# One core, decay mixing and a routed low-rank layer: the first group's router sums in 64 rows, and other places for its sigmoid, some additions, copies and weight chunks

## The chip, the core and the metric

One core of a Trainium2 chip runs the whole program. Its engines are PE (TensorE, the matrix products), DVE (VectorE), ACT (ScalarE), POOL (GpSimd) and SP (SyncE, which here only issues transfers); each works through its own instructions in order and waits on semaphores. The metric is the device time of one execution in microseconds (us).

## What is computed

The reference, cut to what matters (4 sequences of 1024 steps, 1024 channels, 16 experts of rank 16, a router with 64 hidden values):

```python
ekv = exp(min(k, 30)) * v              # k = v = fside
nf, df = forward decaying sums of ekv, ek over time
nb, db = the same backward in time
euk = exp(min(u + k, 30))
base = sigmoid(r) * ((nf + nb - ekv + euk * v) / max(df + db - ek + euk, 1e-8))
y = base * (0.8 + 0.2 * tf)            # r = x
h = silu(y @ rw1.T + rb1)
logits = (h @ rw2.T + rb2)[:, :16] + gates
coeff = softmax of the two largest logits, at their places
out = x + y @ W.T + bias + einsum(B, (y @ A.T) * coeff)
```

## The kernel before

**Units.** A unit is 128 channels of one sequence over its 1024 steps; there are 32, eight for each sequence (CB is 8). Step s of each engine's main loop deals with unit s and with what is left of unit s - 1. On DVE a unit costs two forward scans (`forward`, `forward_num`), two backward ones (`backward_den`, `backward_num`), `p2`, `sum_den`, `scale_e` for the next unit and, in the next step, `ratio`. ACT takes the exponentials (`exp_k`, `exp_uk`), `sigmoid_r`, and with `inverse` a logarithm and an exponential for the reciprocal, and rounds y to its high part (`split_hi`). The sigmoid is in another function table than the rest, so that ACT loads a table ahead of it and again behind it (`exps`). POOL takes the product `p1`, the sum `sum_n`, the gate `gate_n` and the low part (`split_lo`).

**Groups.** A group is 512 steps of one sequence over its eight units; there are eight, G = 0 to 7, and two of them share a sequence. PE multiplies each y, held as a high and a low part, with weights that are held so too: three products of 512 columns (`three`). For a group it makes the router's sums (`hid`), the two low-rank banks (`low_rank`), the base of outputs j = 0 to 7 (`base`), and the experts' share (`expert`). Between them stands the routing: `hidden`, a sigmoid and `silu`, then `logits` on PE, `routing` on DVE (with one exponential, `exp_gap`, on ACT), `turn` and `spread` on PE with a copy on ACT between (`copy_turned`), `weigh` on DVE, and `split_wx` on ACT and POOL, on which the experts wait.

**Two forms of the router's sum.** `hid` multiplies the weights' high and low parts side by side, 128 rows in all, in two products for a unit; the two halves must then be added, so ACT copies the low rows out (`low_rows`) and DVE adds them (`hidden`). Group 2 (`SPLIT`) uses `hid_sum` instead: three products into 64 rows, with nothing to add, and ACT takes the sigmoid right from the bank (`sigmoid_sum`).

**The order around it.** Hand-written tables say at which step and place each engine does the groups' work: `silu_at`, `routing_at`, `weigh_at` for DVE; `drains_at` for ACT's copies of finished output banks and `adds_at` for POOL's transfers that add them to the output in memory; `x_adds_at` for POOL's transfers that add x; `hi_steps` and `hi_mid_steps` for ACT's half of the weight chunks' split into high and low (POOL's half follows by `lo_steps`); `parts_at` for ACT's copies of part sums. A part is the sum over the first units of one output of group 0 or 1, made while PE has nothing else; `part_depth` says over how many units. There are four buffers for parts, so part 7 goes where part 3 was, once that is stored.

## Time and profile before

| | |
|---|---|
| median of 3 runs | 663.84 us (662.76 to 664.39) |
| the profiled execution | 663.93 us, span 661.9 us |
| mean granted TensorE clock | 0.977 of full |
| busy share of the span | PE 89%, DVE 77%, ACT 56%, POOL 57% |

The span goes from the first to the last instruction; 2.0 us of the execution's own time lie outside it. Matmuls overlap, so that PE counts as busy while they follow each other without a gap.

### The profile page before, as it was taken

The page shows a single profiled execution, that of the slowest core. Times are in us where ns is not written, and L with a number is a line of the kernel's source. Part 1 is how long each engine was busy: PE and PEld are TensorE (multiplying, and loading weights), DVE is VectorE, ACT ScalarE, POOL GpSimd, SP SyncE. Part 2 cuts the span into 40 slices and gives each one's busy share as a digit, 9 for nine tenths or more (in the row PEclk, how much of TensorE's full clock was granted, in tenths as well). Part 3 has the DMA queues.
Part 4 walks back from the last instruction along what each step waited for, and adds up shares of the span by engine and source line. Part 5 has one row for each costly group of instructions (what it writes and reads, how often), then busy time and mean ns, then how long its engine had stood idle before and what let it go on. Part 6 is the DMA issues. An engine that isn't in the chain of part 4 may idle for free.

```text
span 661.9 us, 6944 instructions
## 1 busy us (share of the span) xinstructions
...
## 2 busy tenths in 40 slices
...
GB/s 199 125 95 190 169 200 182 161 161 111 136 78 92 165 125 65 135 213 247 58 143 44 259 79 50 111 175 175 49 111 64 145 0 96 0 159 0 42 55 80
DMA packets 32097, 78.45 MB, mean 119 GB/s; under 512 B 4608, under 2 KB 4800, under 8 KB 32064
## 3 DMA queue, kind: packets, MB, share of 16 engines
...
q8 instruction: 20, 0.33, 0.2%
...
## 4 chain that ended last, share of the span: by engine, by line
PE 45%; DVE 24%; POOL 11%; ACT 7%; issue 7%; DMA 6%; SPq 0%; POOLq 0%; ACTq 0%; DVEq 0%
PE acc L1041 14%; PE acc L1043 14%; PE acc L1042 14%; DVE mix L836 4%; DVE mix L831 4%; DVE mix L827 4%; DVE mix L858 3%; POOL mix L710 3%; DMA yr<-x_cm 2%; POOL y_lo L720 2%; POOL mix L685 2%; DVE eu L846 2%; DVE yr L865 2%; DVE kv L841 1%; POOL yr L691 1%
## 5 line engine op out<-in xcount | busy, mean ns | idle before, releaser
L1041 PE MATMUL acc<-y_hi,wa_hi 128*128 128x512 f32 x638 | 256.6, 402 | 52.4 <-POOL y_lo L720 46.6
L1042 PE MATMUL acc<-y_lo,wa_hi 128*128 128x512 f32 x638 | 253.5, 397 | 0.0
L1043 PE MATMUL acc<-y_hi,wa_lo 128*128 128x512 f32 x638 | 253.4, 397 | 0.0
L1041 PEld LDWEIGHTS acc<-y_hi,wa_hi 128*128 128x128 f32 x638 | 122.9, 193 | 82.9 <-POOL y_lo L720 48.4
L1043 PEld LDWEIGHTS acc<-y_hi,wa_lo 128*128 128x128 f32 x638 | 122.8, 192 | 26.4
L1042 PEld LDWEIGHTS acc<-y_lo,wa_hi 128*128 128x128 f32 x638 | 122.9, 193 | 25.2
L710 POOL TENSOR_TENSOR mix<-mix,kv 128x1024 f32<-128x1024 f32 x30 | 72.8, 2425 | 70.2 <-DVE mix L814 70.2
L720 POOL TENSOR_TENSOR y_lo<-yr,y_hi 128x1024 fp32r<-128x1024 f32 x31 | 75.5, 2434 | 35.5 <-ACT y_hi L440 35.4
L879 DVE SCALAR_TENSOR_TENSOR xo<-acc,bias_sb,xo 128x512 f32<-128x512 f32 x48 | 35.3, 738 | 73.6 <-PE acc L1043 73.5
L733 POOL TENSOR_TENSOR wx_lo<-xa,wx_hi 128x512 fp32r<-128x512 f32 x16 | 20.4, 1295 | 112.2 <-ACT wx_hi L528 112.2
L685 POOL TENSOR_TENSOR mix<-mix,kv 128x1024 f32<-128x1024 f32 x31 | 75.0, 2419 | 4.0 <-DVE mix L858 4.0
L836 DVE TENSOR_TENSOR_SCAN mix<-d_ps,mix 128x1023 f32<-128x1023 f32 x32 | 74.5, 2330 | 3.3 <-ACT mix L452 3.3
L827 DVE TENSOR_TENSOR_SCAN mix<-d_ps,mix 128x1024 f32<-128x1024 f32 x32 | 72.9, 2279 | 5.1 <-POOL mix L710 5.0
L691 POOL TENSOR_TENSOR yr<-mix,yr 128x1024 f32<-128x1024 f32 x31 | 74.2, 2393 | 4.5 <-DVE yr L865 2.2
L858 DVE TENSOR_TENSOR_SCAN mix<-d_ps,mix 128x1023 f32<-128x1023 f32 (+1 forms) x32 | 73.7, 2303 | 0.0
L831 DVE TENSOR_TENSOR_SCAN mix<-d_ps,mix 128x1024 f32<-128x1024 f32 x32 | 72.5, 2267 | 0.0
L475 ACT ACTIVATE eu<-eu,tiny 128x1024 f32<-128x1024 f32 (+1 forms) x32 | 34.3, 1073 | 38.2 <-DVE eu L846 38.0
L429 ACT ACTIVATE eu<-kv,u_sb 128x1024 f32<-128x1024 f32 x32 | 35.8, 1118 | 27.4 <-DVE yr L865 27.3
L1041 PE MATMUL acc<-wx_hi,wb_hi 128*128 128x512 f32 x128 | 50.0, 391 | 0.6 <-POOL wx_lo L733 0.6
L1042 PE MATMUL acc<-wx_lo,wb_hi 128*128 128x512 f32 x128 | 49.8, 389 | 0.0
L1043 PE MATMUL acc<-wx_hi,wb_lo 128*128 128x512 f32 x128 | 49.8, 389 | 0.0
L440 ACT ACTIVATE y_hi<-yr 128x1024 fp32r<-128x1024 f32 x31 | 32.6, 1052 | 24.1 <-POOL yr L691 24.0
(128 smaller groups left out, 731.6 us busy)
## 6 DMA issues: line engine op xcount, KB each, us to landing
kv<-f_cm SPq DMA_DIRECT2D x32, 512.0 KB, 3.6
yr<-x_cm SPq DMA_DIRECT2D x32, 512.0 KB, 3.5
out<-xo SPq DMA_DIRECT2D x64, 256.0 KB, 3.7
xo<-x_cm SPq DMA_DIRECT2D x48, 256.0 KB, 3.9
out<-x_cm POOLq DMA_DIRECT2D x8, 512.0 KB, 7.9
out<-xo POOLq DMA_DIRECT2D x16, 256.0 KB, 5.9
xa<-w_base SPq DMA_DIRECT2D x5, 512.0 KB, 3.5
xo<-w_base SPq DMA_DIRECT2D x3, 512.0 KB, 4.8
```

The source lines that it names most:

```text
L429: nc.scalar.activation(eu[:], kv[:, g % 2, :], ACT.Exp, bias=u_sb[:, g % CB:g % CB + 1]).then_inc(euk_ready, 1)
L685: nc.gpsimd.tensor_tensor(n_of(g)[:, t], num_of(g)[:, t], kv[:, g % 2, t], ALU.add).then_inc(n_ready, 1)
L691: nc.gpsimd.tensor_tensor(yr[:, g % 2, t], n_of(g)[:, t], yr[:, g % 2, t], ALU.mult).then_inc(y_ready, 1)
L710: nc.gpsimd.tensor_tensor(num_of(g), den_of(g), kv[:, g % 2, :], ALU.mult).then_inc(p1_ready, 1)
L720: nc.gpsimd.tensor_tensor(slots(y_lo, g), yr[:, g % 2, :].rearrange("p (h t) -> p h t", h=2), slots(y_hi, g).bitcast(fp32), ALU.subtract). ...
L827: nc.vector.tensor_tensor_scan(den_of(g), decay(g, T), den_of(g), 0.0, ALU.mult, ALU.add).then_inc(den_fwd, 1)
L831: nc.vector.tensor_tensor_scan(num_of(g), decay(g, T), num_of(g), 0.0, ALU.mult, ALU.add).then_inc(num_fwd, 1)
L836: nc.vector.tensor_tensor_scan(rev(den_of(g)), decay(g, T - 1), rev(den_of(g)), den_of(g)[:, T - 1:T], ALU.mult, ALU.add).then_inc(den_bwd, 1)
L858: nc.vector.tensor_tensor_scan(a[:, stop - 1::-1], decay(g, stop), a[:, stop - 1::-1], a[:, stop:stop + 1], ALU.mult, ALU.add).then_inc(nu ...
L1041: nc.tensor.matmul(out_ap, wh, yh, start=start, stop=False)
L1042: nc.tensor.matmul(out_ap, wh, yl, start=False, stop=False)
L1043: return nc.tensor.matmul(out_ap, wl, yh, start=False, stop=stop)
```

## The change

Group 0 now makes its router sums with `hid_sum`, and takes the way of group 2 from there: no `low_rows`, no `hidden`; the sigmoid from the bank stands in step 8, ahead of unit 8's `inverse`; `silu` follows `scale_e`. Its routing stands behind unit 8's last scan and ahead of `ratio`, `weigh` ahead of unit 9's `forward_num`. ACT and POOL have an order of their own in step 9. On PE the base of output 1 stands behind `logits`. Elsewhere: parts 8 and 9 take in five units instead of four, and are copied out later; the router's weight chunks 6 and 8 are converted in the middle of the next step; additions 4 and 12 go behind the next step's `gate_n` (and 6 behind `split_lo`), and the copy of output 14 from step 14 to the end of step 13.

```diff
-        hi_steps = [[1], [2], [3, 4], [5, 6], [7, 8], [9], [10], [11]]
-        hi_mid_steps = [[], [], [], [], [], [], [], [], [12]]
+        hi_steps = [[1], [2], [3, 4], [5], [7], [9], [10], [11]]
+        hi_mid_steps = [[], [], [], [], [6], [8], [], [], [12]]
...
-        part_depth = [HALF - 1] * 5 + [HALF] * 5 + [HALF + 2] * 6
+        part_depth = [HALF - 1] * 5 + [HALF] * 3 + [HALF + 1] * 2 + [HALF + 2] * 6
...
-        adds_at = {(CB + 2, AFTER_GATE): (0, 1), (CB + 2, AFTER_LO): (1, 5), (CB + 3, AFTER_GATE): (5, 7),
-                   (CB + 3, AFTER_LO): (7, 8), (CB + 5, AFTER_GATE): (8, 10), (CB + 5, AFTER_LO): (10, 13),
+        adds_at = {(CB + 2, AFTER_GATE): (0, 1), (CB + 2, AFTER_LO): (1, 4), (CB + 3, AFTER_GATE): (4, 6),
+                   (CB + 3, AFTER_LO): (6, 8), (CB + 5, AFTER_GATE): (8, 10), (CB + 5, AFTER_LO): (10, 12),
...
+                if s == CB + 1:
+                    copy_xa(0)
+                    exp_gap(0)
+                    sigmoid_r(s)
+                    exps()
+                    copy_turned(0)
+                    exp_uk(s)
+                    scale_end_den(s)
+                    split_wx(0)
+                    split_hi(s - 1)
+                    scale_end_num(s)
+                    exp_k(s + 1)
+                    inverse(s)
+                    drains(s, AFTER_INVERSE)
+                    continue
...
-                if q == 0:
+                if q == 0 and G == 0:
+                    sigmoid_sum(G)
+                    exps()
+                elif q == 0:
                     low_rows(G)
...
+                if s == CB + 1:
+                    sum_n(s - 1)
+                    for n in chunks_at(lo_steps, s):
+                        weights_lo(n)
+                    for j in tiles(x_adds_at, s, AFTER_GATE):
+                        add_x(j)
+                    gate_n(s - 1)
+                    for j in tiles(x_adds_at, s, AFTER_LO):
+                        add_x(j)
+                    split_wx(0)
+                    split_lo(s - 1)
+                    p1(s + 1)
+                    continue
...
             def hid_sum(G, kc):
                 yh, yl = y_of(G, kc)
-                three(acc[0:HID, banks[G][0], :], wr[:, kc, 0:HID], wr[:, kc, HID:2 * HID], yh, yl, kc == 0, False)
+                last = three(acc[0:HID, banks[G][0], :], wr[:, kc, 0:HID], wr[:, kc, HID:2 * HID], yh, yl, kc == 0, kc == CB - 1)
+                if kc == CB - 1:
+                    last.then_inc(hid_done, 1)
...
                         unit_in(G, kc)
                         pe.wait_ge(w_lo_ready, router_a_chunk[kc] + 1)
-                        hid(G, kc)
+                        hid_sum(G, kc)
```

In ACT's program, step 8 and the start of step 9 before (L495 is `low_rows`, L475 and L477 `inverse`, L499 the group's sigmoid, L464 `sigmoid_r`, L429 `exp_uk`, L510 `copy_xa`; a table load without a name is `exps` or belongs to the line's sigmoid):

```order
125 L491 ACTIVATE wb_hi<-xo 128x1024 [waits w_in0]
126 L495 COPY fan<-acc 64x512 [waits hid_done]
127 L475 ACTIVATE eu<-eu,tiny 128x1024 [waits den_ready]
128 L477 ACTIVATE eu<-eu,log_gain_g 128x1024 [waits log_ready]
129 L499 ACT_TABLE_LOAD
130 L499 ACTIVATE acc<-fan 64x512 [waits z_ready]
131 L464 ACTIVATE yr<-yr 128x1024 [waits r_in1]
132 L554 ACT_TABLE_LOAD
133 L429 ACTIVATE eu<-kv,u_sb 128x1024 [waits ratio_ready,k_in1]
134 L510 COPY xa<-acc 128x512 [waits w_lo_ready,xa_done]
135 L510 COPY xa<-acc 128x512
```

and now (L504 the sigmoid from the bank, L476 and L478 `inverse`, L511 `copy_xa`, L515 `exp_gap`, L465 `sigmoid_r`, L524 `copy_turned`):

```order
125 L492 ACTIVATE wb_hi<-xo 128x1024 [waits w_in0]
126 L504 ACT_TABLE_LOAD
127 L504 ACTIVATE fan<-acc,rb_sb 64x512 [waits hid_done]
128 L555 ACT_TABLE_LOAD
129 L476 ACTIVATE eu<-eu,tiny 128x1024 [waits den_ready]
130 L478 ACTIVATE eu<-eu,log_gain_g 128x1024 [waits log_ready]
131 L511 COPY xa<-acc 128x512 [waits w_lo_ready,xa_done]
132 L511 COPY xa<-acc 128x512
133 L515 ACTIVATE ex<-gap 128x4 [waits gap_ready]
134 L465 ACT_TABLE_LOAD
135 L465 ACTIVATE yr<-yr 128x1024 [waits r_in1]
136 L555 ACT_TABLE_LOAD
```

The copy is gone, the sigmoid stands ahead of the logarithm between two table loads, and `sigmoid_r` of unit 9 with two loads of its own stands between the copies of the low-rank banks and `copy_turned`, with `exp_uk` behind all of them.

In DVE's program the same place before (L814 `scale_e`, L884 `hidden`, L858 `backward_num`, L865 `ratio`, L893 `silu`, L827 `forward`, L904 to L938 `routing`, L831 `forward_num`, L945 `weigh`):

```order
88 L814 TENSOR_SCALAR mix<-mix,delta_g 128x1024
89 L884 SCALAR_TENSOR_TENSOR fan<-acc,rb_sb,fan 64x512
90 L858 SCALAR_TENSOR_TENSOR mix<-d_ps,mix 128x1023
91 L865 SCALAR_TENSOR_TENSOR yr<-eu,limit_g,yr 128x1024
92 L893 TENSOR_TENSOR fan<-acc,fan 64x512
93 L827 SCALAR_TENSOR_TENSOR mix<-d_ps,mix 128x1024
94 L904 TENSOR_TENSOR lg<-acc,rbg 128x64
...
109 L938 TENSOR_TENSOR cat<-d_ps,cat 128x8x16
110 L831 SCALAR_TENSOR_TENSOR mix<-d_ps,mix 128x1024
111 L945 TENSOR_TENSOR xa<-acc,xa 128x512 x2
```

and now (L920 `silu`, L888 `backward_num`, L934 to L968 `routing`, L895 `ratio`, L857 `forward`, L975 `weigh`, L861 `forward_num`):

```order
88 L844 TENSOR_SCALAR mix<-mix,delta_g 128x1024
89 L920 SCALAR_TENSOR_TENSOR fan<-acc,rb_sb,fan 64x512
90 L888 SCALAR_TENSOR_TENSOR mix<-d_ps,mix 128x1023
91 L934 TENSOR_TENSOR lg<-acc,rbg 128x64
...
106 L968 TENSOR_TENSOR cat<-d_ps,cat 128x8x16
107 L895 SCALAR_TENSOR_TENSOR yr<-eu,limit_g,yr 128x1024
108 L857 SCALAR_TENSOR_TENSOR mix<-d_ps,mix 128x1024
109 L975 TENSOR_TENSOR xa<-acc,xa 128x512 x2
110 L861 SCALAR_TENSOR_TENSOR mix<-d_ps,mix 128x1024
```

The routing's 22 instructions (16 rows) went ahead of `ratio` and `forward`, and `weigh` ahead of `forward_num`; one addition of 512 columns is gone.

In POOL's program, from step 10 on, before (L746 are the additions to the output, L720 `split_lo`, L710 `p1`, L685 `sum_n`, L691 `gate_n`):

```order
68 L746 DMA out<-xo 128x512 [waits part_stored0,drained]
69 L720 TENSOR_TENSOR y_lo<-yr,y_hi 128x2x512 [waits hi_ready]
70 L746 DMA out<-xo 128x512 [waits part_stored1,drained]
71 L746 DMA out<-xo 128x512 [waits part_stored2,drained]
72 L746 DMA out<-xo 128x512 [waits part_stored3,drained]
73 L746 DMA out<-xo 128x512 [waits part_stored0,x_added4,drained]
74 L710 TENSOR_TENSOR mix<-mix,kv 128x1024 [waits den_ready,e_scaled]
75 L685 TENSOR_TENSOR mix<-mix,kv 128x1024 [waits p2_ready,num_bwd]
76 L691 TENSOR_TENSOR yr<-mix,yr 128x1024 [waits ratio_ready,n_ready]
77 L746 DMA out<-xo 128x512 [waits part_stored1,x_added5,drained]
```

and now (L763 the additions, L737 `split_lo`, L727 `p1`, L702 `sum_n`, L708 `gate_n`):

```order
68 L763 DMA out<-xo 128x512 [waits part_stored0,drained]
69 L737 TENSOR_TENSOR y_lo<-yr,y_hi 128x2x512 [waits hi_ready]
70 L763 DMA out<-xo 128x512 [waits part_stored1,drained]
71 L763 DMA out<-xo 128x512 [waits part_stored2,drained]
72 L763 DMA out<-xo 128x512 [waits part_stored3,drained]
73 L727 TENSOR_TENSOR mix<-mix,kv 128x1024 [waits den_ready,e_scaled]
74 L702 TENSOR_TENSOR mix<-mix,kv 128x1024 [waits p2_ready,num_bwd]
75 L708 TENSOR_TENSOR yr<-mix,yr 128x1024 [waits ratio_ready,n_ready]
76 L763 DMA out<-xo 128x512 [waits part_stored0,x_added4,drained]
77 L763 DMA out<-xo 128x512 [waits part_stored1,x_added5,drained]
```

Three additions instead of four stand between `split_lo` of unit 9 and `p1` of unit 11; the fourth went behind `gate_n` of unit 10. Step 13 changes in the same way.

## Rows read from the trace of the kernel before

**Rows 1.** The page, issued additions: KB each, median us to landing.

```profile
out<-x_cm POOLq DMA_DIRECT2D x8, 512.0 KB, 7.9
out<-xo POOLq DMA_DIRECT2D x16, 256.0 KB, 5.9
```

**Rows 2.** Stretches: length, busy PE, PEld, DVE, ACT, POOL, then clock, DMA.

```profile
402.44:661.90 259.46, 255.86 (x1139) 209.16 (x1139) 130.23 (x178) 78.61 (x94) 76.75 (x36) 1.00 0.26 84
258.39:386.23 127.84, 125.80 (x557) 102.99 (x557) 122.75 (x113) 80.36 (x90) 84.83 (x40) 1.00 0.49 144
...
125.00:130.00 5.00, 3.46 (x9) 2.70 (x10) 4.47 (x5) 3.73 (x5) 5.00 (x3) 0.67 0.42 120
```

**Rows 3.** Timeline of PE: start, length, operation [idle before <-releaser].

```profile
126.54 0.65 PE L1072 MATMUL acc<-y_hi,wr 128*128 128x512 f32 x1 [2.34 <-POOL y_lo L720]
...
146.45 0.50 PE L1041 MATMUL acc<-wx_hi,wb_hi 128*128 128x512 f32 x1 [0.28 <-POOL wx_lo L733]
...
184.30 1.06 PE L1110 MATMUL acc<-rw_sb,fan 64*128 64x16 f32 x8
...
258.39 0.50 PE L1041 MATMUL acc<-y_hi,wa_hi 128*128 128x512 f32 x1 [1.20 <-DVE xa L945]
...
402.44 0.50 PE L1125 MATMUL acc<-cat_t,expand_r 32*128 32x512 f32 x2 [1.37 <-ACT cat_t L523]
```

**Rows 4.** Groups of PE by shape: busy us, mean ns of one | idle before.

```profile
L1073 PE MATMUL acc<-y_lo,wr 128*128 128x512 f32 x56 | 22.0, 393 | 0.0
...
L1042 PE MATMUL acc<-y_lo,wr 128*64 128x512 f32 x7 | 2.7, 392 | 0.0
```

**Rows 5.** Timelines of POOL and ACT, units 3 and 4.

```profile
69.38 2.35 POOL L720 TENSOR_TENSOR y_lo<-yr,y_hi 128x1024 fp32r<-128x1024 f32 x1 [0.61 <-ACT y_hi L440]
...
77.65 0.31 ACT L486 ACTIVATE wr<-xo 128x128 fp32r<-128x128 f32 x1 [1.76 <-DMA xo<-w_router_a]
77.86 0.62 ACT L487 ACTIVATE wa_hi<-xo 128x512 fp32r<-128x512 f32 x1
```

**Rows 6.** Timeline of DVE around the first group's routing.

```profile
128.27 0.74 DVE L884 SCALAR_TENSOR_TENSOR fan<-acc,rb_sb,fan 64x512 f32<-64x512 f32 x1 [0.53 <-ACT fan L495]
...
135.35 0.23 DVE L904 TENSOR_TENSOR lg<-acc,rbg 128x64 f32<-128x64 f32 x1
...
139.00 0.29 DVE L938 TENSOR_TENSOR cat<-d_ps,cat 128x128 fp32r<-128x128 f32 x1
...
142.42 1.29 DVE L945 TENSOR_TENSOR xa<-acc,xa 128x512 f32<-128x512 f32 x2 [0.93 <-PE acc L1125]
```

**Rows 7.** Timeline of ACT: a table load and what follows it.

```profile
130.49 1.28 ACT L499 ACT_TABLE_LOAD   x1
131.78 0.59 ACT L499 ACTIVATE acc<-fan 64x512 f32<-64x512 f32 x1
```

**Rows 8.** Timeline of POOL, units 9 and 10.

```profile
143.85 2.54 POOL L733 TENSOR_TENSOR wx_lo<-xa,wx_hi 128x512 fp32r<-128x512 f32 x2 [0.52 <-ACT wx_hi L528]
...
159.73 3.09 POOL L746 DMA_DIRECT2D out<-xo  x3
165.56 0.88 POOL L746 DMA_DIRECT2D out<-xo  x1 [2.74 <-issue]
```

**Rows 9.** Timeline of DVE, units 11 to 14: its waits.

```profile
168.89 2.29 DVE L827 TENSOR_TENSOR_SCAN mix<-d_ps,mix 128x1024 f32<-128x1024 f32 x1 [3.04 <-POOL mix L710]
...
189.07 0.17 DVE L918 TENSOR_SCALAR d_ps<-ex 128x4 f32<-128x4 f32 x1 [1.74 <-ACT ex L514]
...
217.14 2.29 DVE L827 TENSOR_TENSOR_SCAN mix<-d_ps,mix 128x1024 f32<-128x1024 f32 x1 [0.65 <-POOL mix L710]
...
226.77 0.75 DVE L814 TENSOR_SCALAR mix<-mix,delta_g 128x1024 f32<-128x1024 f32 x1 [0.66 <-ACT mix L423]
```

**Rows 10.** Timelines of SP and ACT: load and sigmoid of unit 12.

```profile
177.85 0.33 SPq L338 DMA_DIRECT2D yr<-x_cm  x1
...
184.27 1.06 ACT L464 ACTIVATE yr<-yr 128x1024 f32<-128x1024 f32 x1 [1.62 <-DMA yr<-x_cm]
```

More of the change, by code:

```diff
@@ L159, in decay_mix_with_routed_lora_channel_major @@
         PBUF = 4
[L160 removed]
+        part_depth = [HALF - 1] * 5 + [HALF] * 3 + [HALF + 1] * 2 + [HALF + 2] * 6
         PART_EXP_K, PART_CHUNK, PART_END = range(3)
[L162 removed]
+        parts_at = {(3, PART_CHUNK): (0, 3), (4, PART_CHUNK): (3, 5), (4, PART_END): (5, 8), (5, PART_END): (8, 10),
                     (6, PART_END): (10, 13), (7, PART_EXP_K): (13, 16)}
@@ L184, in decay_mix_with_routed_lora_channel_major @@
                      (CB + 2, AFTER_INVERSE): (6, 7), (CB + 3, AFTER_HI): (7, 8), (CB + 4, AFTER_INVERSE): (8, 10),
-                     (CB + 5, AFTER_HI): (10, 12), (CB + 5, AFTER_EXP_K): (12, 13), (CB + 5, AFTER_INVERSE): (13, 14),
-                     (CB + 6, AFTER_HI): (14, 16)}
+                     (CB + 5, AFTER_HI): (10, 12), (CB + 5, AFTER_EXP_K): (12, 13), (CB + 5, AFTER_INVERSE): (13, 15),
+                     (CB + 6, AFTER_HI): (15, 16)}
         AFTER_GATE, AFTER_LO = range(2)
@@ L203, in decay_mix_with_routed_lora_channel_major @@
         ends_at = {first_step(G) + (3 if G == SPLIT else 4): G for G in range(SPLIT, GROUPS)}
-        hidden_at = {(first_step(G), AFTER_SUM if G == 4 else AFTER_SCALE): G for G in range(GROUPS) if G != SPLIT}
-        silu_at = {(first_step(G) + 1, AFTER_RATIO): G for G in range(GROUPS) if G not in (SPLIT, 4)}
-        silu_at |= {(THIRD, AFTER_FWD): SPLIT, (FIFTH, AFTER_BWD_NUM): 4}
-        routing_at = {(first_step(G) + 1, AFTER_FWD): G for G in (0, 1, 5, 6, 7)}
-        routing_at |= {(first_step(3) + 1, AFTER_BWD_DEN): 3}
+        SUMMED = (0, SPLIT)
+        hidden_at = {(first_step(G), AFTER_SUM if G == 4 else AFTER_SCALE): G for G in range(GROUPS) if G not in SUMMED}
+        silu_at = {(first_step(G) + 1, AFTER_RATIO): G for G in range(GROUPS) if G not in (0, SPLIT, 4)}
+        silu_at |= {(CB, AFTER_SCALE): 0, (THIRD, AFTER_FWD): SPLIT, (FIFTH, AFTER_BWD_NUM): 4}
+        routing_at = {(first_step(G) + 1, AFTER_FWD): G for G in (1, 5, 6, 7)}
+        routing_at |= {(CB, AFTER_BWD_NUM): 0, (first_step(3) + 1, AFTER_BWD_DEN): 3}
         routing_at |= {(THIRD, AFTER_FWD_NUM): SPLIT, (FIFTH + 1, AFTER_RATIO): 4}
-        weigh_at = {(first_step(G) + 1, AFTER_FWD_NUM): G for G in (0, 4, 5, 6, 7)}
-        weigh_at |= {(first_step(1) + 1, AFTER_BWD_DEN): 1, (THIRD, AFTER_BWD_DEN): SPLIT, (first_step(3) + 1, AFTER_SCALE): 3}
+        weigh_at = {(first_step(G) + 1, AFTER_FWD_NUM): G for G in (4, 5, 6, 7)}
+        weigh_at |= {(CB + 1, AFTER_FWD): 0, (first_step(1) + 1, AFTER_BWD_DEN): 1, (THIRD, AFTER_BWD_DEN): SPLIT, (first_step(3) + 1, AFTER_SCALE): 3}
         def summed(G):
-            return G + 1 - (G > SPLIT)
+            return G + 1 - sum(1 for g in SUMMED if g < G)
         def quarter(s):
@@ L618, in _ @@
                     scale_end_num(s)
-                if routed and G == 0:
-                    split_wx(G)
                 if routed and G == 3:
@@ L633, in _ @@
                     drain_part(p)
-                if routed and G not in (0, 3):
+                if routed and G != 3:
                     split_wx(G)
@@ L888, in silu @@
                 dve.wait_ge(zs_ready, G + 1)
-                if G == SPLIT:
+                if G in SUMMED:
                     nc.vector.scalar_tensor_tensor(out=z, in0=acc[0:HID, banks[G][0], :], scalar=rb1_sb[:, 0:1],
@@ L1154, in _ @@
                 parts([p], range(4))
-            parts(range(10, 13), [4])
+            parts(range(8, 13), [4])
             for p in range(13, 15):
@@ L1188, in _ @@
                         pe.wait_ge(w_lo_ready, router_a_chunk[kc] + 1)
-                        hid(G, kc)
+                        hid_sum(G, kc)
                         for a in range(2):
@@ L1198, in _ @@
                     base(G, 0, CB - 1)
-                    bank_in(G, 4)
-                    for kc in range(base_from(G, 1), CB):
-                        base(G, 1, kc)
                     pe.wait_ge(late_in, 16 * 8)
@@ L1262, in _ @@
                     logits(G)
-                if G not in (0, SPLIT):
+                if G != SPLIT:
                     bank_in(G, 4)
```

3 lines of the change are left out of this document (1 added, 2 removed).

## The prediction

> **What bounds the kernel now.** I read the stretches first, then PE's waits, then DVE's. From 402.4 us to its last product PE has no gap: 1139 products, busy 255.9 us, which is 0.225 us from one to the next [rows 2]. PE enters that stretch behind a wait of 1.37 us for group 4's routing [rows 3]. So the end is that moment plus a block that the change does not touch, and the question is how much sooner PE gets there. From 258.4 to 386.2 PE is busy too, 125.8 of 127.8 us, and DVE 122.8 [rows 2]: the two are close, but PE enters there as well behind a wait for DVE, 1.20 us for `weigh` of group 2 [rows 3]. Ahead of that PE waits for DVE and POOL again and again. The chain of units on DVE sets the time up to 402 us, and a stall taken from it before 258 us should arrive at the end whole, as long as PE keeps up. Where DVE waits itself is in rows 6 and 9: 0.93 us in `weigh` of group 0, 3.04 in `forward` of unit 11, 1.74 in group 1's routing, 0.65 and 0.66 at unit 14.
>
> **Weight chunks and parts (steps 3 to 6).** ACT waited 1.76 us for chunk 8 to land, and POOL 0.61 us in step 4 for a y_hi that ACT gave late because of chunk 6 [rows 5]. Both waits for landings go. But POOL is full in these steps, so in step 4 only its 0.61 us is gained. In step 5 the conversion of chunk 8, 0.93 us [rows 5], now stands behind `exp_k` of unit 6, POOL's two subtractions for it wait for it, and `p1` of unit 6 behind them. And the copy of part 7 still waits until part 3 is stored, which is hardly sooner. Sum: 0.93 - 0.61, a loss of 0.3. Bounds: a gain of 1.8 if the whole wait of 1.76 us comes free, a loss of 0.9 if POOL's 0.61 is not kept.
>
> **More products on PE.** `hid_sum` adds eight. A product into 64 rows takes what one into 128 takes, 392 against 393 ns [rows 4], so 8 x 0.225 = 1.8 us, seven of them ahead of unit 7, where PE waited 2.34 us [rows 3]: 1.6 us are covered and 0.8 left. Six products of parts 8 and 9 move from behind unit 12 to ahead of unit 5; without cover there they would cost 1.4 us.
>
> **Group 0's routing (steps 8 and 9).** All in the times of the old trace. Unit 7's y_lo comes at 126.5. Three products at the low clock (9 products, so 8 spacings, in 3.46 us busy: 0.43 us from one to the next [rows 2]) end the sums at 128.0. The sigmoid takes 0.6 [rows 7], `silu` 0.7: 129.4. Before, `hidden` ended at 129.0 [rows 6]: 0.4 later. `backward_num` goes to 131.6. PE has twelve products after 126.5, eight at the low clock, and starts `logits` at 130.9; 1.06 [rows 3] makes 132.0. The routing took 135.35 to 139.29 [rows 6], 3.9 us: 136.0. `ratio` and `forward` (1.2, taken like `weigh` [rows 6], and 2.2 [rows 9]) go to 139.4. Meanwhile PE makes 27 products from 132.0, 6.1 us, to 138.1, then `turn`, the copy and `spread`, some 1.8: 139.9. `weigh` can start there, against 142.42 [rows 6], so 2.5 sooner, and is done at 141.1; its wait of 0.93 falls to 0.5. Then the split for the experts: POOL does `sum_n`, the last expert chunk and an addition of x, then `gate_n`, which needs `ratio` at 137.2, to 139.6, two additions of x to 141.6, and `split_wx` in 2.5 [rows 8]: 144.1. PE's first expert product started at 146.45 [rows 3]. **PE gains 2.3 us here.** DVE itself gains less: `backward_den` of unit 9 starts at 143.3 instead of 143.6; at the full clock it would be 142.1.
>
> What ACT gains by `low_rows` it loses twice over, since `sigmoid_sum` stands between two table loads of its own, so there are two more, 2.6 us. `copy_turned` is behind them at 137.1, and the turned routing comes at 138.6, so they are covered by PE's 27 products with 1.5 us to spare; `exp_uk` of unit 9, behind the copy, is wanted by `backward_den` only at 142. The table load took 1.28 us from 130.49, and the next instruction began at 131.78 [rows 7]: nothing is paid beside it. The Trainium skill, "ScalarE: Activation LUTs", What ACT_TABLE_LOAD costs, has 1283 ns and besides a drain of about 1380 ns for each switch, 2.66 us in all. The row shows the first and no drain. By the rule the four loads ahead of `copy_turned` would make 5.5 us more, of which 1.5 are covered; by the row nothing, and I go by the row.
>
> `split_lo` of unit 8 moves behind `split_wx`, to 146.5, some 5 us later. Only `load_r` of unit 10 waits for that; PE wants unit 8 for group 2 alone, far behind.
>
> **POOL's additions (steps 10 to 12).** In step 10 three additions go out in a row, and the fourth is held 2.74 us with no releaser shown, then `p1` of unit 11 follows [rows 8] and DVE waits 3.04 us [rows 9]. 165.56 is 5.8 us behind the first of the three, and such an addition takes 5.9 to land [rows 1]: it is held by those in flight, I take it. With that addition behind `gate_n` 6 us later, nothing holds it, and the 3.04 us go. DVE would then be 3.3 us ahead or more at unit 12's `forward`. But it needs group 1's logits there, which PE had at 184.30 + 1.06 = 185.36 [rows 3], after a stretch without gap from the experts on. PE is only 2.3 ahead, so **the routing of group 1 begins 2.3 us sooner** and no more.
>
> Inside it DVE waited 1.74 us for an exponential [rows 9], for ACT was held by `sigmoid_r` of unit 12, whose data was issued at 177.85 and used at 184.27 [rows 10]. That issue waits for `split_lo` of unit 10, which now comes about 4 us sooner (one addition less in front, and `p1` of unit 11 3 us sooner). **1.7 us** go.
>
> **Steps 13 and 14.** The same cut once more: one addition less ahead of `p1` of unit 14 removes the wait of 0.65, and that with one copy less in ACT's step 14 (output 14 is copied a step sooner, when ACT had time) the wait of 0.66 for `exp_k` [rows 9]. **1.3 us.**
>
> **The sum.** 663.9 for the profiled execution, 0.1 above the median. + 0.3 - 2.3 - 1.7 - 1.3 = - 5.0: 658.9. A measurement of this kernel tells about 0.3%, or 2 us, from no change.
>
> **Rivals.**
> - **As summed, 658.9**, itself 657.3 to 660.7: 52 in 100. More than that (the full clock at unit 7 and the whole of the chunk wait gained), 656 or less: 5.
> - **The clock takes part of it, 660.6**: 17. PE would reach the experts at 143.1 and wait a microsecond or more, 2.5 if the clock was up, where it waited 0.28 before [rows 3]. After the wait of 2.34 us at unit 7 its clock was at the low level, mean 0.67 over the next 3.5 us [rows 2]. Eight products at that level cost 8 x 0.2 = 1.7 us. Against it: PE is fuller ahead of that wait than it was. The Trainium skill, "TensorE: Matmul & The Clock Gate", The HAM clock gate, says that idleness throttles the array and activity releases it; by this rule the price is the same 1.7.
> - **The hold in POOL is not by number, 662.2**: 10. If it was something else than transfers in flight, and only moves, 3.04 and 0.65 stay, unit 12's data comes late and 1.74 stays: 0.3 - 1.4 - 0.66 = - 1.7.
> - **Given back behind 258 us, 661.4**: 9. That stretch has loads and stores between DVE's steps, and PE idles only 2 us in it [rows 2]; half the gain could end in its waits. Against it: PE enters it behind DVE.
> - **Slower: the x additions hold POOL, up to 670.4**: 5. Two of them now stand ahead of `split_wx`, 512 KB each with 7.9 us to landing [rows 1]. If each had to wait for the one before, the split would come 9.2 us later than it did, and 9.2 - 1.7 - 1.3 + 0.3 = + 6.5. It ends slower from a hold of 5 us on; one of 2.7 us as in rows 8 leaves a gain of 2.
> - **The drain of a table load, 662.9**: 2. Four microseconds in front of `copy_turned` put the experts 1.6 us later than before: 1.6 - 1.7 - 1.3 + 0.3 = - 1.1. This is the rule of the first page cited; the row speaks against it.
>
> Faster: 52 + 5 + 17 and half of 9, 0.78. Slower: 0.06. The rest, 0.16, lies within 0.3%. The range has to take in the clock and the hold in POOL on one side, the full gain at unit 7 and in the chunks on the other (2.3 to 3.5 for PE, 1.8 for the chunks, not both whole): 656.6 to 662.2.
>
> **What would show it.** After, DVE should have no wait at `forward` of unit 11, a wait of some 1 to 2 us for the logits of group 1 where there was none, and none for the exponential behind it. PE's first expert product stands near 144.4, after a wait of about 1 us. POOL shows no hold in step 10. PE's stretch without gap begins near 397.5. The step most likely wrong is PE's time to the experts: it rests on products, ACT and POOL meeting within a microsecond. If the first two units after the chunks show a wait of DVE for `p1` of unit 6 longer than 1.5 us, the first term is wrong.

## The result, and the profile after

| | before | after |
|---|---|---|
| median beside each other | 662.93 us (5 runs) | 657.32 us (5 runs) |
| ratio | | 0.9905, 95% interval 0.9882 to 0.9929 |
| once more each, in two of the experiments' rounds | 663.74, 662.41 | 657.55 (0.9896), 656.48 (0.9899) |
| the profiled execution | 663.93 us, span 661.9 | 657.03 us, span 654.9 |

The change makes the kernel 5.6 to 6.2 us faster. The ratio and its interval are the measurement's own and not the quotient of the two medians, 0.9915; by the ratio it is 6.3 us, 4.7 to 7.8. Forecast were 658.9 us and a range of 656.6 to 662.2: right in sign and inside the range, 1.6 us too slow. Two terms were mis-sized, and part of what the two profiles differ by is chance (below). One of run 1's twelve executions took 774.88 us at a granted clock of 0.76 and is not counted below.

On the page after, the engines, the clock and the additions:

```profile
PE 586.5 (90%) x2562; PEld 472.7 (72%) x2562; DVE 506.1 (77%) x562; ACT 372.1 (57%) x446; POOL 374.6 (57%) x190
...
PEclk9977899999989989999999999999999999999999
...
out<-xo POOLq DMA_DIRECT2D x16, 256.0 KB, 7.1
```

PE has 8 products more and is busy 586.5 us of 654.9. The slices of the clock around unit 7 are up, one near 190 us is down. An addition to the output takes 7.1 us to land where it took 5.9 [rows 1].

PE's stretch without gap, from behind its last wait to its last product, and the four microseconds behind four of its waits (columns as in [rows 2]):

```profile
395.47:654.90 259.43, 255.83 (x1139) 209.21 (x1139) 130.23 (x178) 78.67 (x94) 76.75 (x36) 1.00 0.25 84
125.60:129.60 4.00, 3.99 (x21) 3.09 (x21) 3.26 (x4) 3.96 (x4) 3.71 (x2) 1.00 0.59 160
142.70:146.70 4.00, 3.93 (x17) 3.27 (x18) 4.00 (x5) 1.03 (x1) 2.72 (x3) 1.00 0.80 155
190.90:194.90 4.00, 4.00 (x12) 3.21 (x13) 4.00 (x5) 2.33 (x4) 2.69 (x3) 0.64 0.02 4
238.30:242.30 4.00, 3.97 (x11) 2.95 (x12) 2.68 (x2) 3.32 (x5) 3.87 (x3) 0.59 0.00 0
```

The block at the end is what it was, 259.43 us for 1139 products against 259.46 [rows 2], and starts at 395.47 instead of 402.44. So the end moved by what this moment moved, 6.97 us in these two executions. PE's rows that answer to [rows 3]:

```profile
125.61 0.45 PE L1071 MATMUL acc<-y_hi,wr 128*64 128x512 f32 x1 [0.69 <-POOL y_lo L737]
...
142.77 0.50 PE L1071 MATMUL acc<-wx_hi,wb_hi 128*128 128x512 f32 x1 [1.38 <-POOL wx_lo L750]
...
190.89 0.79 PE L1071 MATMUL acc<-y_hi,wa_hi 128*128 128x512 f32 x1 [2.69 <-DVE xa L975]
...
238.33 0.69 PE L1091 MATMUL acc<-y_hi,wr 128*64 128x512 f32 x1 [2.20 <-ACT y_hi L449]
...
395.47 0.50 PE L1157 MATMUL acc<-cat_t,expand_r 32*128 32x512 f32 x2 [1.37 <-ACT cat_t L524]
```

The wait at unit 7 fell from 2.34 to 0.69 us and left the clock up. PE's first expert product stands at 142.77 (146.45 before), behind a wait of 1.38. DVE around the first group's routing, at unit 11, in group 1's routing and behind it [rows 6, 9]:

```profile
127.54 0.74 DVE L920 SCALAR_TENSOR_TENSOR fan<-acc,rb_sb,fan 64x512 f32<-64x512 f32 x1 [0.74 <-ACT fan L504]
...
130.46 0.19 DVE L934 TENSOR_TENSOR lg<-acc,rbg 128x64 f32<-128x64 f32 x1
...
137.68 1.26 DVE L975 TENSOR_TENSOR xa<-acc,xa 128x512 f32<-128x512 f32 x2
...
162.70 2.29 DVE L857 TENSOR_TENSOR_SCAN mix<-d_ps,mix 128x1024 f32<-128x1024 f32 x1
...
181.73 0.22 DVE L934 TENSOR_TENSOR lg<-acc,rbg 128x64 f32<-128x64 f32 x1 [2.33 <-PE acc L1142]
...
242.33 0.74 DVE L920 SCALAR_TENSOR_TENSOR fan<-acc,rb_sb,fan 64x512 f32<-64x512 f32 x1 [1.32 <-ACT fan L504]
...
375.80 2.35 DVE L866 TENSOR_TENSOR_SCAN mix<-d_ps,mix 128x1023 f32<-128x1023 f32 x1
```

`forward` of unit 11 has no wait, the logits of group 1 have one of 2.33, the exponential none, unit 14 none. POOL in steps 9 and 10 (L771 are the additions of x, L763 those to the output), against [rows 8]:

```profile
138.20 1.98 POOL L771 DMA_DIRECT2D out<-x_cm  x2
139.29 3.43 POOL L750 TENSOR_TENSOR wx_lo<-xa,wx_hi 128x512 fp32r<-128x512 f32 x2
...
157.16 3.07 POOL L763 DMA_DIRECT2D out<-xo  x3
159.39 3.27 POOL L727 TENSOR_TENSOR mix<-mix,kv 128x1024 f32<-128x1024 f32 x1
```

Three additions go out and `p1` follows at once.

### The profile page after: what moved, and what is told of

It reads as the page before. It is cut to its first block, busy times and chain, and to the rows that moved or that the text cites. A ratio compares the mean times of both kernels' runs of the same rounds, so it can differ in the third digit from the quotient of the medians.

```text
span 654.9 us, 6960 instructions
## 1 busy us (share of the span) xinstructions
PE 586.5 (90%) x2562; PEld 472.7 (72%) x2562; DVE 506.1 (77%) x562; ACT 372.1 (57%) x446; POOL 374.6 (57%) x190
## 4 chain that ended last, share of the span: by engine, by line
PE 47%; DVE 26%; POOL 11%; issue 6%; ACT 6%; DMA 4%; SPq 0%; POOLq 0%; DVEq 0%; ACTq 0%
PE acc L1071 15%; PE acc L1073 14%; PE acc L1072 14%; DVE mix L866 4%; DVE mix L861 4%; DVE mix L857 4%; DVE mix L888 3%; DMA yr<-x_cm 2%; POOL mix L727 2%; POOL y_lo L737 2%; DVE eu L876 2%; DVE yr L895 2%; POOL mix L702 2%; POOL yr L708 2%; DVE kv L871 1%
## 5 line engine op out<-in xcount | busy, mean ns | idle before, releaser
L727 POOL TENSOR_TENSOR mix<-mix,kv 128x1024 f32<-128x1024 f32 x30 | 74.8, 2495 | 69.2 <-DVE mix L844 69.2
L737 POOL TENSOR_TENSOR y_lo<-yr,y_hi 128x1024 fp32r<-128x1024 f32 x31 | 76.7, 2475 | 33.8 <-ACT y_hi L441 33.8
L702 POOL TENSOR_TENSOR mix<-mix,kv 128x1024 f32<-128x1024 f32 x31 | 76.8, 2478 | 3.8 <-DVE mix L888 3.8
L708 POOL TENSOR_TENSOR yr<-mix,yr 128x1024 f32<-128x1024 f32 x31 | 74.5, 2405 | 4.4 <-DVE yr L895 2.2
L857 DVE TENSOR_TENSOR_SCAN mix<-d_ps,mix 128x1024 f32<-128x1024 f32 x32 | 73.1, 2285 | 2.6 <-POOL mix L727 2.5
L888 DVE TENSOR_TENSOR_SCAN mix<-d_ps,mix 128x1023 f32<-128x1023 f32 (+1 forms) x32 | 73.9, 2309 | 0.0
L861 DVE TENSOR_TENSOR_SCAN mix<-d_ps,mix 128x1024 f32<-128x1024 f32 x32 | 72.7, 2272 | 0.0
L476 ACT ACTIVATE eu<-eu,tiny 128x1024 f32<-128x1024 f32 (+1 forms) x32 | 34.3, 1073 | 39.6 <-DVE eu L876 39.3
```

What stands on the lines that cost most here:

```text
L702: nc.gpsimd.tensor_tensor(n_of(g)[:, t], num_of(g)[:, t], kv[:, g % 2, t], ALU.add).then_inc(n_ready, 1)
L708: nc.gpsimd.tensor_tensor(yr[:, g % 2, t], n_of(g)[:, t], yr[:, g % 2, t], ALU.mult).then_inc(y_ready, 1)
L727: nc.gpsimd.tensor_tensor(num_of(g), den_of(g), kv[:, g % 2, :], ALU.mult).then_inc(p1_ready, 1)
L737: nc.gpsimd.tensor_tensor(slots(y_lo, g), yr[:, g % 2, :].rearrange("p (h t) -> p h t", h=2), slots(y_hi, g).bitcast(fp32), ALU.subtract). ...
L857: nc.vector.tensor_tensor_scan(den_of(g), decay(g, T), den_of(g), 0.0, ALU.mult, ALU.add).then_inc(den_fwd, 1)
L861: nc.vector.tensor_tensor_scan(num_of(g), decay(g, T), num_of(g), 0.0, ALU.mult, ALU.add).then_inc(num_fwd, 1)
```

## The experiments

Single microseconds are hard to tell by medians, but a profile shows where they are. This table has, for each profile, the time in us from the forward scan of one unit to that of another, so that what happens outside a stretch doesn't count in it. The medians come from four rounds. The kernel before had 662.93 us in that of the first two rows, 663.26 beside runs 1 to 4, 663.74 beside the second profile of after, runs 6 and 7 and the first of v1, and 662.41 beside the third of after, run 5, v1 again and v2; each ratio below is to the kernel before in the run's own round.

| kernel | 4 to 7 | 8 to 10 | 10 to 11 | 12 to 13 | 13 to 15 | 16 to 17 | 24 to 25 | median |
|---|---|---|---|---|---|---|---|---|
| before | 43.26 | 34.08 | 16.67 | 20.16 | 27.42 | 20.69 | 20.97 | 662.93 |
| after | 42.29 | 32.44 | 13.07 | 20.87 | 26.09 | 21.07 | 20.04 | 657.32 |
| after, second profile | 42.26 | 32.42 | 13.06 | 20.90 | 26.38 | 20.95 | 20.76 | 657.55 |
| after, third profile | 42.34 | 32.42 | 13.06 | 20.75 | 26.21 | 20.99 | 20.28 | 656.48 |
| chunks and parts alone | 42.47 | 33.09 | 16.45 | 20.21 | 27.23 | 20.83 | 20.75 | 662.41 |
| group 0 alone | 42.74 | 32.43 | 17.91 | 20.06 | 27.36 | 21.96 | 20.88 | 662.46 |
| additions alone | 42.83 | 33.79 | 13.59 | 21.58 | 26.01 | 20.68 | 21.36 | 660.58 |
| two additions, then three | 42.72 | 33.76 | 13.56 | 21.44 | 27.21 | 22.05 | 20.97 | 662.09 (one run) |
| after, hold put back | 42.30 | 32.42 | 17.53 | 20.16 | 26.09 | 20.70 | 20.86 | 660.37 |
| after, routing behind `forward` | 42.36 | 33.60 | 15.44 | 21.48 | 26.24 | 20.82 | 20.79 | 661.22 |
| after, `split_lo` first | 42.48 | 32.43 | 17.65 | 21.48 | 27.47 | 20.69 | 20.27 | 662.45 |
| after, split first (v1) | 42.43 | 32.43 | 13.06 | 19.68 | 26.01 | 20.70 | 20.50 | 657.67 |
| v1 again | 42.23 | 32.43 | 13.05 | 19.67 | 26.21 | 21.01 | 20.34 | 655.81 |
| v1 and logits sooner (v2) | 43.21 | 32.43 | 13.14 | 19.41 | 26.02 | 20.69 | 19.89 | 655.13 |

**1. Chunks and parts alone.** Before, with

```diff
-        hi_steps = [[1], [2], [3, 4], [5, 6], [7, 8], [9], [10], [11]]
+        hi_steps = [[1], [2], [3, 4], [5], [7], [9], [10], [11]]
...
-            parts(range(10, 13), [4])
+            parts(range(8, 13), [4])
```

and the other lines of these tables in the change's diff.

> The kernel before with only the chunk and part tables of the change (chunks 6 and 8 converted in the middle of the next step, parts 8 and 9 over five units and copied a place later). By the prediction's first term the units behind step 6 come 0.3 us later, 663.2 against 662.9. By what the changed kernel's trace shows (unit 6's forward scan 1.0 us sooner, unit 5's 0.64) they come 1.0 us sooner, and nothing eats that before the end: 661.9. The rival to both: the 1.0 us of the changed kernel came from another part of the change, then unit 6 starts at 91.5 as before and the time is 662.9. PE's first expert product: 145.4 by the second, 146.7 by the first.

Ratio 0.9983 (0.9967 to 0.9999). From unit 4 to unit 7 it takes 42.47 us; three kernels with the old tables (group 0 alone, additions alone, two then three) take 42.72 to 42.83, but the profiled execution of before 43.26. So by unit 7 the edit is worth a gain of 0.3 to 0.5 us, and the other half of the 0.97 us that the profile after shows there was chance in the profile of before: ACT waited 2.12 us for chunk 6 to land, and 1.17 to 1.43 in those three. The prediction's loss of 0.3 has the wrong sign. The new tables have such an execution too, that of v2, with 43.21 us: ACT's copy of part 7 waited 2.63 us there for the store of part 3, and 1.72 in after.

Stretch 8 to 10 is shorter as well, 33.09 us against 34.08 before and 33.76 to 33.79 in the two other kernels with before's order of group 0 (runs 3 and 5), and PE's first expert product stands at 144.96, sooner than either value that was expected. No edit lies there. What differs most is PE's clock, behind its wait for ACT's copy of a low-rank bank. Before:

```profile
136.36 0.50 PE L1041 MATMUL acc<-y_hi,wa_hi 128*128 128x512 f32 x1 [1.04 <-ACT xa L510]
...
136.36:140.36 4.00, 4.00 (x11) 3.15 (x12) 3.76 (x21) 1.66 (x4) 4.00 (x3) 0.58 0.70 130
```

and in run 1, behind a wait of 0.66 us:

```profile
135.35:139.35 4.00, 3.55 (x17) 2.71 (x18) 3.69 (x23) 1.74 (x5) 4.00 (x3) 1.00 0.72 133
```

Run 3 waited 2.09 us there and had 0.57, as run 5 had.

**2. Group 0 alone.** The kernel after with the old tables of chunks, parts, copies and additions.

> The kernel before with only the new way of group 0 (router sums in 64 rows, sigmoid from the bank, new orders in steps 8 and 9). PE's first expert product comes 2.7 us sooner, at 143.7 (the prediction had 2.3 with a low clock at unit 7). The hold in POOL's additions of step 10 is left where it was relative to the additions, so DVE keeps only its own gain of 1.6 us at unit 10 and the routing of group 1 begins 1.6 sooner, not 2.7: now DVE is the later one. The waits of 1.74 for the exponential and of 0.65 and 0.66 at unit 14 stay. Time 661.3 (minus 1.6). Rival: PE's 2.7 us arrive whole, 660.2. Rival: the hold takes all, unit 11's scan at 168.9 as before, 662.9.

Ratio 0.9987 (0.9968 to 1.0006): it can't be told from no change. Its stretch 8 to 10 is as short as after's, and PE's first expert product stands at 143.22. But the next stretch takes 1.24 us more than before's. The hold in POOL has grown, from 2.74 to 3.98 us, and DVE's wait for `p1` from 3.04 to 4.87 (timelines of POOL and DVE):

```profile
157.60 3.08 POOL L763 DMA_DIRECT2D out<-xo  x3
164.66 0.87 POOL L763 DMA_DIRECT2D out<-xo  x1 [3.98 <-issue]
...
168.00 2.29 DVE L857 TENSOR_TENSOR_SCAN mix<-d_ps,mix 128x1024 f32<-128x1024 f32 x1 [4.87 <-POOL mix L727]
```

The first of the three additions, issued at 157.60 and so 2.13 us sooner than before's, took 6.8 us to land where that took 5.5; the hold ends about 0.3 us behind the landing. So of the 1.6 us expected at unit 10, which are there, 1.24 went in this execution to a longer landing, and from unit 16 to 17 another 1.27 behind a fallen clock (0.50 over 4 us behind a wait of 2.96). Whether they go in others, one profile can't tell; the interval of the times holds the expected 0.9975 as well as no change.

**3. Additions alone.** Before, with the change's lines in `adds_at` and `drains_at`.

> The kernel before with only the new places of additions 4, 6, 12 and of the copy of output 14. If the fourth addition in a row was held by those in flight, the hold of 2.74 us is gone and unit 11's forward scan comes 3.0 us sooner, near 165.9. PE has group 1's logits at 185.36 as before, so the routing begins at 185.4 behind a new wait of about 3 us: nothing gained there. The exponential's wait of 1.7 and the two waits at unit 14, 1.3 together, go: 3.0 less, 659.9, or up to 0.7 more than that if the stretch behind 258 us gives some back. Rival, the prediction's: the hold was not by number and only moves, then the routing starts as before, the 1.74 stays and the gain is at most 0.7: 662.3.

Ratio 0.9957 (0.9942 to 0.9972), 2.7 us less. The hold is gone (stretch 10 to 11: 3.08 shorter), DVE waits 3.15 us for the logits instead, the exponential's wait is gone, and unit 13 to 15 is 1.41 shorter. DVE's timeline at unit 11 and at the routing:

```profile
164.97 2.28 DVE L827 TENSOR_TENSOR_SCAN mix<-d_ps,mix 128x1024 f32<-128x1024 f32 x1
...
184.61 0.23 DVE L904 TENSOR_TENSOR lg<-acc,rbg 128x64 f32<-128x64 f32 x1 [3.15 <-PE acc L1110]
```

**4. The hold put back.** After, with

```diff
-(CB + 2, AFTER_LO): (1, 4), (CB + 3, AFTER_GATE): (4, 6), (CB + 3, AFTER_LO): (6, 8)
+(CB + 2, AFTER_LO): (1, 5), (CB + 3, AFTER_GATE): (5, 7), (CB + 3, AFTER_LO): (7, 8)
```

> The changed kernel with the additions of steps 10 and 11 where they were before (four in a row behind the low part of unit 9, then two, then one). In flight theory: the hold comes back, 2.7 us, and unit 11's forward scan comes 3.0 to 3.6 us later than in the changed kernel, near 166. DVE waited 2.3 us for group 1's logits there, which covers most: the routing starts 0.7 to 1.3 later. The load of unit 12's x is issued 3 us later, and the wait of 1.7 for the exponential returns: together 2.4 to 3.0 more than the changed kernel, 659.7 to 660.3. Rival: with the earlier PE and POOL no hold appears, and the time is that of the changed kernel, 657.3.

660.37 us, ratio 0.9951 (0.9932 to 0.9970), 3.1 above the first median of after, as by the two ratios. The hold is 3.62 us (timelines of POOL and DVE):

```profile
157.11 3.08 POOL L763 DMA_DIRECT2D out<-xo  x3
163.81 0.87 POOL L763 DMA_DIRECT2D out<-xo  x1 [3.62 <-ACT xo L548]
...
167.13 2.29 DVE L857 TENSOR_TENSOR_SCAN mix<-d_ps,mix 128x1024 f32<-128x1024 f32 x1 [4.49 <-POOL mix L727]
...
187.34 0.17 DVE L948 TENSOR_SCALAR d_ps<-ex 128x4 f32<-128x4 f32 x1 [1.75 <-ACT ex L515]
```

The issue of the first of the three, in the view of transfers (KB, us to landing):

```profile
out<-xo POOLq DMA_DIRECT2D x1, 256.0 KB, 6.4
```

157.11 and 6.4 make 163.5, and again the hold ends 0.3 behind it. The profile names ACT's copy as releaser. That copy ended at 162.86, and in the other traces with a hold nothing is named.

**5. Two additions, then three.** Before, with `(CB + 2, AFTER_GATE): (0, 2), (CB + 2, AFTER_LO): (2, 5)`.

> The kernel before with addition 1 ahead of the low part of unit 9 in step 10, so that two additions go out, then the low part, then three, instead of one and four. Theory, the hold ends when the first of three in flight has landed: addition 0 lands about 4 us behind its issue (at 160.0), addition 1 issued at 157 lands about 162; when the last of the three comes to be issued, near 162.8, only two or three are in flight, so no hold or one below 0.5 us, and p1 of unit 11 starts 2.5 us sooner. Rival, the fifth addition of the step is what is held, wherever it stands: the hold stays near 2.7 us. Rival, the fourth addition's buffer or its x is late: output 4's addition is held until 165.6.

POOL's timeline:

```profile
155.26 1.81 POOL L746 DMA_DIRECT2D out<-xo  x2
...
158.84 2.41 POOL L746 DMA_DIRECT2D out<-xo  x2
161.50 0.87 POOL L746 DMA_DIRECT2D out<-xo  x1 [0.24 <-issue]
162.06 2.73 POOL L710 TENSOR_TENSOR mix<-mix,kv 128x1024 f32<-128x1024 f32 x1
```

The second of the first pair by itself, and its issue in the view of transfers:

```profile
155.87 1.20 POOL L746 DMA_DIRECT2D out<-xo  x1
...
out<-xo POOLq DMA_DIRECT2D x1, 256.0 KB, 5.3
```

The same five additions before the same `p1`, and the hold is 0.24 us. That second addition was issued at 155.87 and took 5.3 us, to 161.2: the fifth went out 0.3 us behind that. In all five traces with such a hold no more than three additions are in flight; the next one holds POOL until the oldest has landed. The two rivals on record, that the fifth addition is held wherever it stands and that output 4's waits for its own data until 165.6, are both out.

**6. Routing behind `forward`.** After, with

```diff
-        routing_at |= {(CB, AFTER_BWD_NUM): 0, ...
-        weigh_at |= {(CB + 1, AFTER_FWD): 0, ...
+        routing_at |= {(CB + 1, AFTER_FWD): 0, ...
+        weigh_at |= {(CB + 1, AFTER_FWD_NUM): 0, ...
```

> The changed kernel with group 0's routing and weighing at DVE's old places (routing behind forward of unit 9, weighing behind its forward_num), the rest as changed. Theory: the order on DVE is what made the experts early. The routing then starts behind ratio and forward, 3.4 us later, near 134.0, the weighing near 139.9 instead of 137.7, the split starts 1.4 to 2.2 later than in the changed kernel, and PE's first expert product stands at 144.2 to 145; DVE waits for group 1's logits, so all of it arrives: 658.8 to 659.5. Rival: the 64 rows and the earlier sigmoid did it, and PE's first expert product stays within 0.5 us of 142.8: 657.3 to 657.8.

661.22 us, ratio 0.9960 (0.9946 to 0.9974): 3.7 above after in the same round. PE's first expert product comes at 146.87, 4.1 later and outside the 144.2 to 145 expected. From unit 8's scan it is 29.42 us, more than before's 28.31. The clock has a part in it, since it fell behind a wait of 2.59 for the routing. PE's timeline:

```profile
138.77 0.42 PE L1149 MATMUL acc<-ident_r,cat 128*64 128x128 f32 x4 [2.59 <-DVE cat L968]
...
141.59 0.79 PE L1071 MATMUL acc<-y_hi,wa_hi 128*128 128x512 f32 x1 [0.77 <-DVE xa L975]
...
146.87 0.63 PE L1071 MATMUL acc<-wx_hi,wb_hi 128*128 128x512 f32 x1
```

The last row has no wait: PE came late to it, with the clock at 0.50 from 141.60 on (10 products in 4 us). POOL's split was done at 144.82. So an estimate for the order on DVE by itself is 2.0 us, which is most of what PE gains at the experts, and the other 2.0 or so are the clock's.

**7. `split_lo` first.** After, with `split_lo(s - 1)` ahead of `split_wx(0)` in POOL's step 9.

> The changed kernel with the low part of unit 8 back in front of the split for the experts on POOL. The split ends about 2.7 us later, PE's first expert product stands near 145.5 behind a wait of about 4 us. Theory of the clock (a rival of the prediction): behind so long a wait the granted clock is at its low level for some eight products, which cost 1.7 us more, so group 1's routing begins 4.4 later than in the changed kernel and the time is 661.7. Rival: the clock stays up behind this wait as it did behind that of 1.38, then 2.7 later: 660.0. Third: DVE's own chain, not PE, is what the time hangs on, then it stays at 657.3.

662.45 us, ratio 0.9977 (0.9961 to 0.9993), 4.9 above after. PE waits 4.11 us. The stretch behind it:

```profile
145.80:149.80 4.00, 3.95 (x9) 3.14 (x10) 4.00 (x4) 2.86 (x3) 3.10 (x2) 0.50 0.33 130
```

Its clock is at 0.50 of full, 1.2 GHz: 9 products, where after has 17. Then it is ACT that waits, and DVE for ACT:

```profile
145.85 0.79 PE L1071 MATMUL acc<-wx_hi,wb_hi 128*128 128x512 f32 x1 [4.11 <-POOL wx_lo L750]
...
148.81 0.69 ACT L548 ACTIVATE xo<-acc,bias_sb 128x512 f32<-128x512 f32 x1 [0.61 <-PE acc L1073]
151.32 0.69 ACT L548 ACTIVATE xo<-acc,bias_sb 128x512 f32<-128x512 f32 x1 [1.82 <-PE acc L1073]
152.71 0.69 ACT L548 ACTIVATE xo<-acc,bias_sb 128x512 f32<-128x512 f32 x1 [0.69 <-PE acc L1073]
...
156.99 2.35 DVE L866 TENSOR_TENSOR_SCAN mix<-d_ps,mix 128x1023 f32<-128x1023 f32 x1 [2.57 <-ACT mix L453]
...
166.41 1.29 DVE L895 SCALAR_TENSOR_TENSOR yr<-eu,limit_g,yr 128x1024 f32<-128x1024 f32 x1 [1.82 <-ACT eu L478]
```

ACT's copies of outputs 0 to 2 stand ahead of `exp_uk` of unit 10 and wait 0.61, 1.82 and 0.69 us for the experts; DVE then waits 2.57 and 1.82 for ACT. So late experts cost DVE directly, not only through group 1's logits. This way was in none of my expectations.

**8. Split first (v1).** After, with `split_wx(0)` ahead of the two additions of x in POOL's step 9.

> The changed kernel with POOL's split for the experts ahead of the two additions of x in step 9. In the changed kernel the two additions took 1.98 us from 138.20 and the split ended at 142.72, though ACT had the first high part by about 139.0. Without them in front it should end near 141.6, and PE's first expert product stand there, 1.1 us sooner behind a wait of 0.3. DVE waits 2.33 us for PE at group 1's logits, so all of it arrives: 656.2. Rival: POOL was held by something else than the additions, or DVE's wait is not PE's to shorten (the logits wait for the sigmoid of unit 15's group instead): 657.3. On the slower side: the additions, now behind, stand in front of the low part of unit 8 and of p1 of unit 10, which would cost up to 1.

PE's first expert product stands at 141.96 behind a wait of 0.28, and stretch 12 to 13 is 1.2 us shorter than after's. The median did not show it (657.67, ratio 0.9906, against 657.55 in the same round), so it ran again beside after.

> The variant with the split for the experts first, unchanged, once more, since its median of six (657.67) and its profile (span 1.2 and 1.8 us shorter than the two of the changed kernel) did not agree. By the profile 1.1 to 1.3 below the changed kernel, 656.3; by the median no difference.

> The changed kernel once more on the same chip as its two variants, so that they are compared with it directly: 657.5 by its two medians so far (657.32, 657.55).

655.81 (0.9889, 0.9868 to 0.9911) against 656.48: 0.7 less, six runs each, from 655.59 to 656.18 and from 656.17 to 656.93. Since the first round had it 0.1 slower, the times alone don't prove the gain; the stretch shows it in both profiles.

**9. Logits sooner (v2).** v1, with nine of group 1's low-rank products behind its logits (shown), and `exp_gap(1)` ahead of `copy_xa(1)`:

```diff
                         for kc in range(first):
+                            if G == 1 and a == 1 and kc == CB - 3:
+                                logits(G)
                             low_rank(G, a, kc)
```

> The changed kernel with the split for the experts first (as in the variant before it), and besides group 1's logits on PE ahead of the last nine low-rank products, and ACT's exponential for group 1's routing ahead of the copies of the low-rank banks. In that variant DVE waited 1.27 us for these logits; silu was done at 177.4, so PE can start them at 177.8 instead of 179.8, DVE starts the routing at 179.6 instead of 180.9, the exponential is ready by 181.0 and wanted at 181.4. Theory: DVE is the later engine from there to 250 us, so 1.3 more arrives at the end: 2.0 to 2.4 us below the changed kernel, 655.3. Rival: the weighing of group 1 then waits for spread on PE, whose time does not move (186.8 plus 0.5), and for the copies of the banks; it has 0.6 us to spare, so no more than 0.5 lost. Rival: PE, busy 98 to 99 in 100 from 250 us on, can't take it up: then the time stays at the variant's, 656.3.

655.13 us, ratio 0.9866 (0.9840 to 0.9893); all of its five runs (653.02 to 655.36) lie below after's six of the same chip. It is the fastest version of this study, 1.35 below after. Of the 1.27 us that DVE waited for the logits it gained 0.26 (stretch 12 to 13); the rest of the 0.68 that its median lies below v1's is not placed. Timelines of DVE and ACT:

```profile
180.19 0.19 DVE L936 TENSOR_TENSOR lg<-acc,rbg 128x64 f32<-128x64 f32 x1
...
183.03 0.17 DVE L950 TENSOR_SCALAR d_ps<-ex 128x4 f32<-128x4 f32 x1 [1.00 <-ACT ex L515]
...
179.38 1.06 ACT L465 ACTIVATE yr<-yr 128x1024 f32<-128x1024 f32 x1 [2.03 <-DMA yr<-x_cm]
...
182.81 0.19 ACT L515 ACTIVATE ex<-gap 128x4 f32<-128x4 f32 x1
```

DVE starts the routing without a wait, and then waits 1.00 for the exponential, since `sigmoid_r` of unit 12 waited 2.03 for its data. The next wait took the place of the one removed.

## Why the prediction was right, and where it was off

- **What bounds the kernel: right.** The block behind the last wait kept its length within 0.03 us, and of the 6.8 us gained by unit 16's scan all arrived at the end but for 0.75 us (0.38 in stretch 16 to 17, 0.37 from unit 20 to 21), which a chance of 0.93 the other way made up for (stretch 24 to 25, below).
- **Weight chunks and parts, "0.93 - 0.61, a loss of 0.3": wrong sign, a term mis-sized, though inside its bounds.** Runs 1 to 3 and 5 give a gain of 0.3 to 0.5 by unit 7. I charged chunk 8's conversion in full to step 5 and counted the wait for its data in step 4 at nothing, because the copy of part 7 waits there too. After shows both: that copy waits 1.72 us, and DVE waits 0.68 for `p1` of unit 6, where it had no wait in runs 2 and 3; but `scale_e` of the step ahead waits 0.33 where it waited 1.28 in both of them. The sum had the one wait that the edit makes, and not the one that it shortens.
- **More products on PE: covered, right.** PE has eight products more, and its wait at unit 7 is 0.69 us where 0.8 was forecast. It had 0.78 and 0.76 in runs 3 and 5 without these products, though: there the clock fell at unit 5, to 0.66 and 0.62 over the 4 us behind waits of 3.12 and 3.11, and the slower products took up the same time.
- **Group 0's routing, "PE gains 2.3 us here": mechanism right, 2.7 measured** (unit 8's scan to the first expert product: 28.31 before, 25.58 after). The low clock that I assumed behind unit 7 did not come; its wait was 0.69. (The forecast's 0.67 is the mean of 125 to 130 us with the wait in it; behind the wait before it was 0.57.) And not all of the 2.7 is the new order: runs 3 and 5 have 28.0 with before's order, and run 1, where the clock stayed up at the place at which it fell before (136.36), has 27.5. So 1.9 to 2.7 us are group 0's, and up to 0.8 may be the clock's. The table loads cost 1.28 us each and nothing beside: one at 132.15, the next instruction at 133.45. "Covered" was the right word: `copy_turned` waited 0.37 for PE, not for them.
- **POOL's additions and "2.3 us sooner and no more": right in kind.** Runs 3 to 5 show that those in flight hold it, run 3 that PE's logits cap it. The routing of group 1 began 3.8 us sooner, not 2.3: 1.0 by unit 7 and 2.7 from there to the experts, all through PE: from its first expert product to that start it is 38.96 us after and 39.04 before. That is the same two terms again. Runs 2 and 3 show what the sum hid: alone, group 0's order gains 0.8 us by the medians, the additions 2.7 and the chunks 0.9, 4.3 together, while all of it makes 5.6 to 6.2. With intervals of 1 us or more on each, the times alone don't prove that difference; the waits show where it comes from. Neither of the two large parts can deliver all of its own alone: without the additions POOL's hold keeps DVE back (4.87 us of wait in run 2), so that PE's lead is idle, and without group 0 PE caps what the additions free (3.15 us of wait in run 3).
- **The exponential, 1.7, and steps 13 and 14, 1.3: right.** From the start of group 1's routing to unit 13 it takes 16.27 us (181.73 to 198.00) where it took 17.96 (185.49 to 203.45), 1.7 less; from unit 13 to 15 1.33 less, in run 3 1.41. The wait of 0.65 for `p1` of unit 14 had mostly the same cause as that of unit 11: before, an addition was held 0.49 us at 213.80, 0.3 behind the landing of the oldest of three.
- **Rival, the clock takes part of it.** At the experts it did not in these three profiles (waits of 1.33 to 1.38, clock 1.00). Run 7 shows its price where it does. Somewhere else it did: behind unit 15 in after, a wait of 2.20 and 0.59 of the clock made `silu` of group 2 wait 1.32 instead of 0.94, which is the 0.38 of stretch 16 to 17. And it had been at work in the kernel before: where PE waited for ACT's copy at 136.36 it was at 0.58, which the forecast left out.
- **Rival, the hold is not by number: false** (runs 3 to 5); the 1.4 in its sum has no working in the prediction. **Rival, given back behind 258 us:** 0.37 us from unit 20 to 21, which one can't tell from chance, for the three profiles of after have 20.78, 20.58 and 20.14 us there and before 20.41. **Rivals, the additions of x and the table's drain:** neither came. The two additions of x stood in front of the split and cost PE 1.1 us (v1), not 9.

Of the profiles' 6.97 us, 0.5 is chance in the profile of before, up to unit 7. Another 0.9 is stretch 24 to 25, where `backward_den` waited 0.97 before and not at all after, though no edit is near: the second profile of after waits 0.75 there, the third 0.24. Behind it is the landing of unit 25's x, for which ACT waited 1.56 us before and 0.57, 1.34 and 0.83 in the three of after. The second profile had been forecast with that unit's scan between 391.4 and 392.3, and it stands at 392.03. Without both it would be 5.6 us, and 6.3 if the 0.75 given back is taken as chance too; the medians have 5.6 to 6.2.
